# An attention and expert kernel: twelve score tiles in one row, one run of value products behind them

## What is computed

```python
q = (query @ w_q.T).reshape(B, T_q, 16, 8)
k = (kv_source @ w_k.T).reshape(B, T_kv, 16, 8)
v = (kv_source @ w_v.T).reshape(B, T_kv, 16, 8)
attn = softmax(einsum('bqhd,bkhd->bhqk', q, k) * 8 ** -0.5, axis=-1)
out = einsum('bhqk,bkhd->bqhd', attn, v).reshape(B, T_q, 128) @ w_o.T
...
x = x + tanh(g_xattn[0]) * xattn(layernorm(x), ctx)
x = x + tanh(g_ffn[0]) * ffn(layernorm(x))
```

## Time and profile before

| | us |
|---|---|
| three runs | 289.75, 289.96, 289.96; median 289.96 |
| the profiled execution | 289.38 |
| its span (first to last instruction) | 287.6 |
| busy: TensorE, VectorE, ScalarE, GpSimd | 275.9 (96%), 214.9 (75%), 181.9 (63%), 97.5 (34%) |
| attention loop, units 0 to 11 | 26.8 to about 166.6 |
| units 12 and 13 | about 166.6 to 189.9 |
| tail, units 14 and 15 | 189.9 to 209 |
| routing and experts | 209 to 287.6 |

### The profile page before, as it was taken

How to read it: one execution, slowest core, us unless ns; L and a number is a source line. 1 busy time by engine, 2 the same in 40 slices (tenths; PEclk the granted TensorE clock), 3 DMA queues, 4 the chain that set the end, 5 groups by cost and what they waited for, 6 DMA issues and landing times.

```text
span 287.6 us, 8051 instructions
## 1 busy us (share of the span) xinstructions
PE 275.9 (96%) x2826; PEld 222.6 (77%) x2826; DVE 214.9 (75%) x420; ACT 181.9 (63%) x370; POOL 97.5 (34%) x113
## 2 busy tenths in 40 slices
PE   7988999999999999999999998999889999999994
PEld 3465878878878888887887887987688788888862
DVE  5678797797877977979679788797256988877761
ACT  2636776687677776777668666566518778775400
POOL 4598732332062043033233201032600755454200
PEclk9999999999999999999999999999999999999999
DMA  7397945943971990892695499100000000000001
GB/s 252 100 206 194 223 107 167 244 132 102 239 203 17 267 252 1 225 236 76 157 233 147 88 219 309 38 0 2 2 2 0 1 2 0 0 1 0 0 0 32
DMA packets 9924, 32.19 MB, mean 112 GB/s; under 512 B 2576, under 2 KB 3088, under 8 KB 9904
## 3 DMA queue, kind: packets, MB, share of 16 engines
q1 hardware_dynamic: 9472, 31.60, 43.1%
q10 hardware_dynamic: 432, 0.33, 0.3%
HBM read 13.26 MB, written 0.23 MB: 47 GB/s over the span
## 4 chain that ended last, share of the span: by engine, by line
PE 87%; DVE 7%; DMA 2%; ACT 1%; issue 1%; POOL 1%; SPq 0%; DVEq 0%; ACTq 0%
PE max_ps L969 16%; PE score_ps L949 14%; PE o_ps L983 14%; PE misc_ps L937 8%; PE misc_ps L931 5%; PE score_ps L1194 3%; PE score_ps L1196 3%; PE score_ps L1195 3%; DVE part_max L704 2%; PE o_ps L1194 2%; PE o_ps L1280 2%; PE o_ps L1195 2%; PE o_ps L1196 2%; PE max_ps L992 2%; PE misc_ps L1107 1%; PE max_ps L999 1%
## 5 line engine op out<-in xcount | busy, mean ns | idle before, releaser
L704 DVE TENSOR_REDUCE part_max<-max_ps 112x1 f32<-112x512 f32 (+1 forms) x192 | 117.3, 670 | 33.4 <-PE max_ps L969 31.5
L515 ACT ACTIVATE probs<-score_ps 128x448 f32<-128x448 f32 x192 | 92.0, 545 | 16.0 <-PE score_ps L949 15.9
L969 PE MATMUL max_ps<-kx,qx 96*112 96x512 f32 (+1 forms) x192 | 81.9, 432 | 2.2 <-DVE part_max L704 1.1
L949 PEld LDWEIGHTS score_ps<-qx,kx 104*128 104x128 f32 (+1 forms) x384 | 69.1, 188 | 10.7 <-issue 2.1
L949 PE MATMUL score_ps<-qx,kx 104*128 104x224 f32 (+1 forms) x384 | 73.7, 276 | 0.6 <-DVE qx L723 0.4
L983 PE MATMUL o_ps<-probs,v_sb 128*32 128x112 f32 (+1 forms) x1536 | 44.5, 261 | 0.6 <-ACT probs L515 0.6
L969 PEld LDWEIGHTS max_ps<-kx,qx 96*112 96x112 f32 x192 | 33.6, 176 | 8.7 <-issue 4.9
L983 PEld LDWEIGHTS o_ps<-probs,v_sb 128*32 128x32 f32 (+1 forms) x1536 | 36.4, 110 | 3.1 <-ACT probs L515 0.8
L366 POOL TENSOR_TENSOR k_low<-k_full,k_high 128x512 fp32r<-128x512 f32 (+1 forms) x21 | 26.2, 1252 | 30.7 <-ACT k_full L498 30.4
L399 POOL TENSOR_TENSOR o_norm<-o_sb,inv_den 128x112 f32 (+1 forms) x15 | 6.3, 423 | 75.8 <-DVE inv_den L730 75.8
L510 ACT ACTIVATE v_sb<-misc_ps 128x512 f32<-128x512 f32 x24 | 14.4, 601 | 27.4 <-PE misc_ps L937 27.4
(11 more groups left out here) (177 smaller groups left out, 369.0 us busy)
## 6 DMA issues: line engine op xcount, KB each, us to landing
kx<-k_high SPq DMA_DIRECT2D x60, 187.5 KB, 5.2
kx<-k_low SPq DMA_DIRECT2D x30, 187.5 KB, 5.1
ctx_sb<-in_ctxT SPq DMA_DIRECT2D x7, 750.0 KB, 5.7
gu_sb<-in_guT SPq DMA_DIRECT2D x8, 512.0 KB, 5.5
dn_sb<-in_dnT SPq DMA_DIRECT2D x8, 256.0 KB, 5.3
ctx_sb<-in_ctxT SPq DMA_DIRECT2D x2, 256.0 KB, 4.3
kx<-k_high SPq DMA_DIRECT2D x4, 123.5 KB, 2.3
kx<-k_high SPq DMA_DIRECT2D x4, 64.0 KB, 2.0
```

The lines of the kernel that those rows point to most:

```text
L515: nc.scalar.activation(probs[:, (KT * h + t) % 8, :], score_ps[:, t % 3, 0:SC // 2], ACT.Exp, scale=SCALE).then_inc(exp_done, 1)
L704: nc.vector.reduce_max(part_max[:, p, c:c + 1], max_ps[0:PC, bank, 0:size], AX.X).then_inc(max_taken, turns)
L949: last = nc.tensor.matmul(score_ps[0:m, t % 3, GC * g:GC * g + GC], kx[0:KR, 2 * par + h, g, 128 * t:128 * t + m], qx[0:KR, par, 2 * h + g ...
L969: nc.tensor.matmul(max_ps[0:PC, bank, 0:size], qx[0:MR, par, 2 * h + p // 2, PC * (p % 2):PC * (p % 2) + PC], kx[0:MR, slot, p // 2, start ...
```

## The change

On TensorE a unit now has its twelve pairs of a maximum product and a score tile in a row, with only the first job (keys) between the sixth and the seventh. Behind the row come the second job, `denominators`, `transpose_max`, both halves of `attend` without anything between them, and then the third job. `probs` has twelve buffers in place of eight, one for each tile, since tile 0's must live until the row's end. VectorE's order follows: twelve maxima (with `negate_max` after the ninth), and the inversion behind the last of them. ScalarE's follows too: six exponentials, the copy of job one, six exponentials, the copy of job two, `o_copy`, and the copy of job three. In the ring the three products of unit u+2 have turns 9 to 11 and the denominators turn 12 (before: 10 to 12, and 6).

The room for four more tiles of `probs` comes from two places. `k_full` holds two chunks of 512 columns in place of 1536 columns, and the third chunk's copy waits until GpSimd has read the first. `expert_sel`, a table of 16x1024, is gone with VectorE's copy that filled it at the start (L748); GpSimd's `select` reads `row_mask` with a broadcast in its place. The tail, the routing and the experts have the same order as before.

```diff
-DEN, NEXT_ROWS, LATER = 6, 13, 10
+DEN, NEXT_ROWS, LATER = 12, 13, 9
...
-        k_full = sb("k_full", [128, KPAD])
+        k_full = sb("k_full", [128, 2, CK])
...
-        probs = sb("probs", [128, 8, GC * 2])
+        probs = sb("probs", [128, KT, GC * 2])
...
-                nc.gpsimd.tensor_copy(expert_now[:, par, :], expert_sel[:, e, :].bitcast(f32)).then_inc(select_ready, 1)
+                nc.gpsimd.tensor_copy(expert_now[:, par, :], bc(row_mask[:, e].unsqueeze(1), [ROWS, 128])).then_inc(select_ready, 1)
...
-            pool.wait_ge(select_all, 1)
+            pool.wait_ge(rows_ready, 1)
...
                 if whole:
-                    nc.scalar.activation(k_full[:, start:start + size], bank[:, 0:size], ACT.Copy).then_inc(k_saved, 1)
+                    if n == 2:
+                        act.wait_ge(k_low_saved, NCH * b + 1)
+                    nc.scalar.activation(k_full[:, n % 2, 0:size], bank[:, 0:size], ACT.Copy).then_inc(k_saved, 1)
...
                 if jobs[0]:
                     jobs[0](i, par, h, 0)
+                for t in range(RUN, KT):
+                    exp_tile(i, par, h, t)
                 if jobs[1]:
                     jobs[1](i, par, h, 1)
-                for t in range(RUN, KT):
-                    exp_tile(i, par, h, t)
+                o_copy(i, par, h)
                 if jobs[2]:
                     jobs[2](i, par, h, 2)
-                o_copy(i, par, h)
...
-                dve.wait_ge(rows_ready, 1)
-                nc.vector.tensor_copy(expert_sel[:, :, :], bc(row_mask[:, :].unsqueeze(2), [16, E, 128])).then_inc(select_all, 1)
...
-                for n in range(RUN):
-                    take_max(ring(u, n), n % 3, AHEAD + n)
-                invert(u - 1, 1 - h, ring(u, DEN), DEN % 3)
-                for n in range(RUN + AHEAD, UM):
-                    take_max(ring(u, n - 2), (n - 2) % 3, n)
+                for n in range(AHEAD, UM):
+                    take_max(ring(u, n - AHEAD), n % 3, n)
                 negate_max(u + 1, ring(u, LATER))
                 for n in range(AHEAD):
                     take_max(ring(u, LATER + n), (LATER + n) % 3, n)
+                invert(u - 1, 1 - h, ring(u, DEN), DEN % 3)
                 max_rows(ring(u, NEXT_ROWS), NEXT_ROWS % 3, *ahead(i, par, h, 1)[1:], turns=2)
...
                 job(i, par, h, 0)
-                denominators(u - 1, 1 - h, ring(u, DEN), DEN % 3)
-                attend(i, par, h, 0)
-                job(i, par, h, 1)
                 for n in range(RUN + AHEAD, UM):
-                    max_scores(*u1, n, ring(u, n - 2), (n - 2) % 3)
+                    max_scores(*u1, n, ring(u, n - AHEAD), n % 3)
                     scores(i, par, h, n - AHEAD)
                 for n in range(AHEAD):
                     max_scores(*u2, n, ring(u, LATER + n), (LATER + n) % 3)
                     scores(i, par, h, KT - AHEAD + n)
+                job(i, par, h, 1)
+                denominators(u - 1, 1 - h, ring(u, DEN), DEN % 3)
+                transpose_max(u + 1, ring(u, NEXT_ROWS), NEXT_ROWS % 3, turns=2)
+                attend(i, par, h, 0)
+                attend(i, par, h, 1)
                 job(i, par, h, 2)
-                transpose_max(u + 1, ring(u, NEXT_ROWS), NEXT_ROWS % 3, turns=2)
-                attend(i, par, h, 1)
```

More of the change, by code:

```diff
@@ L50 @@
 COMB_MADE = 11
+ROWS = 16
 def chunk(n):
@@ L121, in flamingo_block @@
         scratch = sb("scratch", [128, 1])
-        expert_sel = sb("expert_sel", [16, E, 128], f32r)
         expert_now = sb("expert_now", [16, 2, 128], f32r)
@@ L147, in flamingo_block @@
         zeros = k_high[:, 0, 2 * TOK:2 * TOK + 128]
-        x_expert = k_full[:, 0:TOK]
+        x_expert = k_full[:, 0, 0:TOK]
         hact = probs[:, 0:FT, :]
@@ L153, in flamingo_block @@
         yT = o_flat[:, 2 * TOK:3 * TOK]
-        blank = k_full[:, 0:CK]
-        q_full = [k_full[64:MR, CK * (g - 1):CK * (g - 1) + TOK] for g in (2, 3)]
+        blank = k_full[:, 0, :]
+        q_full = [k_full[64:MR, g - 2, 0:TOK] for g in (2, 3)]
         score_ps = pb("score_ps", [128, 3, 512])
@@ L176, in flamingo_block @@
         kx_loaded = [[sem(f"kx_loaded{u}{g}") for g in range(2)] for u in range(4)]
-        consts, mask_ready, select_all, cleared, pool_step = map(sem, ("consts", "mask_ready", "select_all", "cleared", "pool_step"))
+        consts, mask_ready, cleared, pool_step = map(sem, ("consts", "mask_ready", "cleared", "pool_step"))
         scratch_ready = sem("scratch_ready")
@@ L365, in k_rest @@
                 pool.wait_ge(k_saved, 2 * (NCH * b + n + 1))
-                nc.gpsimd.tensor_tensor(k_low[:, par, start:start + size], k_full[:, start:start + size],
+                nc.gpsimd.tensor_tensor(k_low[:, par, start:start + size], k_full[:, n % 2, 0:size],
                                         k_high[:, par, start:start + size].bitcast(f32), ALU.subtract
@@ L514, in exp_tile @@
                 act.wait_ge(scores_done, KT * unit(i, par, h) + t + 1)
-                nc.scalar.activation(probs[:, (KT * h + t) % 8, :], score_ps[:, t % 3, 0:SC // 2],
+                nc.scalar.activation(probs[:, t, :], score_ps[:, t % 3, 0:SC // 2],
                                      ACT.Exp, scale=SCALE).then_inc(exp_done, 1)
@@ L741, in _, with add_masks @@
             dve.wait_ge(x_loaded, 16)
-            def copy_selectors():
+            def add_masks():
                 dve.wait_ge(heads_ready, 1)
@@ L746, in copy_selectors @@
                                         ALU.add).then_inc(mask_ready, 1)
-                dve.wait_ge(rows_ready, 1)
-                nc.vector.tensor_copy(expert_sel[:, :, :], bc(row_mask[:, :].unsqueeze(2), [16, E, 128])).then_inc(select_all, 1)
-            layer_norm(x_sb, 1, 0, NR, copy_selectors)
+            layer_norm(x_sb, 1, 0, NR, add_masks)
             def q_rest(g):
@@ L984, in attend @@
                                                 v_sb[0:m, par, t, VP * p:VP * p + 32],
-                                                probs[0:m, (KT * h + t) % 8, PC * j:PC * j + PC],
+                                                probs[0:m, t, PC * j:PC * j + PC],
                                                 start=(t == 0), stop=(t == KT - 1), skip_group_check=True)
```

## The result

| | before | after |
|---|---|---|
| median of the runs | 289.86 | 294.19 (293.59 to 295.35) |
| ratio | | 1.0159, interval 1.0126 to 1.0192 |
| profiled execution, its span | 289.38, 287.6 | 293.59, 291.9 |
| busy: TensorE, VectorE, ScalarE, GpSimd | 275.9, 214.9, 181.9, 97.5 | 276.0, 215.1, 177.8, 96.8 |

The account below looks back on a forecast made before the run. TensorE was taken to bound the unit, with VectorE slower inside a row of pairs. Loop +0.7, unit 12 -0.7, unit 13 +0.05, start -0.4 gave -0.35 from 289.96: 289.6 us, range 287.0 to 291.8.

Parts of the forecast that it names:

- The small risk inside the forecast: Every second unit: GpSimd's low part touches `negate_max`'s second step, up to 0.2 per unit, 1.2 in six, 290.8; chance 0.06.
- The wait ahead of `transpose_max`: Loop units: TensorE waits 0.35 us for VectorE's longer chain of maxima before `transpose_max`.
- The value run of 2.42: Twelve value tiles in one run take 2.42 us against 2.61 in two runs, 0.19 less per unit.
- Unit 5 plus unit 6, 0.11 more than before: Loop: unit 5 takes 11.72, 0.07 more; unit 6 takes 11.73, 0.04 more; twelve loop units +0.7 us.
- that the third job's copies run into the next unit and no score tile feels it: ScalarE: copies run to about 1.1; first exponential ends some 1.6, the fourth score tile needing it at 1.7.
- Unit 12, -0.7: Unit without a third job: its absence now saves 0.90, giving -0.8 us, less the 0.07.
- Unit 13, +0.05: Unit with three jobs of the same size: 0.05 us longer.
- The start, -0.4: Program start: removing VectorE's copy into `expert_sel` speeds GpSimd's `rstd`, -0.4 us, bounds 0 and 0.6.
- The late context: Slower rival: context load issued later; landing at 7.2 us holds five units 0.6 each, 292.6; chance 0.12.
- The faster rival: Loop: maxima keep up in the long row, the 0.35 wait goes, units cost 11.37, time 284.7; chance 0.17.
- The sum: Whole kernel: + 0.7 - 0.7 + 0.05 - 0.4 = -0.35, a span of 287.3 and median 289.6 us.
- The range: Whole kernel: 287.0 to 291.8 us, halfway to the faster rival and most of the way to the slower.

Follow-up runs that it names:

- the sixth experiment: Changed kernel with the high part of the negated maxima written by a second reduction in place of the cast, GpSimd not held: 290.14 us, ratio 1.0008.
- the fourth experiment: Changed kernel with GpSimd's staging held until that unit's `negate_max` is done, and `transpose_max` behind both halves of the value products: 287.5 us, ratio 0.9917.
- the third experiment: Kernel before with twelve `probs` buffers, two chunks of `k_full` and no `expert_sel`, but the old order on all engines: 289.45 us, ratio 0.9990.
- the fifth: The fourth experiment with SyncE issuing the first key moves ahead of the context's load instead of behind it: 292.68 us, ratio 1.0115.
- seventh experiments: The fifth experiment with the second reduction of the sixth experiment in place of the cast: 292.47 us, ratio 1.0099.
- the ninth: The fourth experiment with the second job behind the ninth pair of the row on TensorE and ScalarE, instead of behind the twelfth: 287.63 us, ratio 0.9911.
- tenth experiments: The ninth experiment with the reduction of the sixth experiment in place of the cast: 284.9 us, ratio 0.9838.
- the eighth experiment: Kernel before, with GpSimd held so that its staging meets `negate_max` in one unit of every two, six in all: 311.13 us, ratio 1.0728.

## Why the prediction was wrong

- **"The small risk inside the forecast" is the step that failed.** It had the right pair of engines. By the Trainium skill, "SBUF — State Buffer", Who interferes with whom, a VectorE copy or cast in a 2-port mode and a GpSimd instruction exclude each other for a whole instruction, and one with two inputs in SBUF contends with GpSimd's reads. The trace agrees, and puts 1.44 and 0.85 us on it for instructions of 0.17 and 0.16; no row names the cast's mode. The prediction named only the rule on two inputs here, though the step that it set beside GpSimd was the cast, which has one input and took 1.27 of the 1.96. The page's other rule there, that `tensor_reduce` never contends on this chip, agrees with the 0.15 of the reduction in the sixth experiment. What failed was the place and the price. The place: I laid out units 5 and 6 and took them for all of the loop, while in unit 0 GpSimd stages and subtracts right behind its clearing of `kx`, 5.60 into the unit, and not behind the normalising, 10.0 into it. In the odd units GpSimd and the cast pass each other by less than the 0.1 that was said: GpSimd's low part ends at 95.77 in unit 5, and the cast starts at 95.78 and takes 0.17. In all six odd units the two are within 0.01. That nothing was held there is luck, not a margin. The price: "up to 0.2" was about the length of the VectorE instruction. The page speaks of one instruction; in the trace the loser waits for the rest of the other's instruction and for the next one behind it too, for both steps together 1.96; and then, in the profiled execution, TensorE's clock adds 1.63.
- **The wait ahead of `transpose_max`**, forecast 0.35: right, 0.23 to 0.33, and the fourth experiment shows that it is this wait which eats the gain of the long run.
- **The value run of 2.42**: right but for 0.04, 2.46 in one run in place of 1.28 + 1.33 = 2.61 in two before.
- **Unit 5 plus unit 6, 0.11 more than before**: measured 0.20 (23.52 against 23.32). Unit 6 came as laid out: `transpose_max` at 8.25 (109.45 - 101.20; forecast 8.31), the unit 11.72 (forecast 11.73). Unit 5 is the longer one, by 0.1: with its start taken as 88.52 + 0.86, the forecast's length of the job before it, `transpose_max` stands at 8.32 in place of 8.26 and the value run is 0.04 longer. One sentence of that step was wrong, that the third job's copies run into the next unit and no score tile feels it. ScalarE's timeline after, at the start of unit 5:

```profile
89.68 0.60 ACT L495 ACTIVATE k_high<-misc_ps 128x512 fp32r<-128x512 f32 x1 [0.74 <-PE misc_ps L929]
...
90.65 2.73 ACT L517 ACTIVATE probs<-score_ps 128x448 f32<-128x448 f32 x6
```

The first of the six exponentials starts at 90.65 only, and TensorE's fourth score tile, due 0.22 behind the maximum product at 90.81, comes at 91.25: 0.22 late. That this is what puts `transpose_max` 0.06 later was not tried.
- **Unit 12, -0.7**: measured -0.84. **Unit 13, +0.05**: measured +0.01.
- **The start, -0.4**: `rstd` did shrink, by 0.45, and in every kernel without the copy, so the copy was in its way and not the operation's first use. How much of it reaches the loop isn't shown: unit 0 starts 0.12 earlier here and 0.34 earlier in the third experiment, kernels with the same code up to there start it between 26.42 and 27.27, and the third experiment gains 0.3 with an interval that includes nothing. I had counted an instruction's saving on the chain as the chain's saving.
- **The late context**, 292.6, decides at a landing of 6.6: the loads land after up to 6.9, and the one above that cost the 0.3. Right as a mechanism, and small in this kernel; the fifth and seventh experiments show its full size.
- **The faster rival**, VectorE not in the way: wrong. TensorE waits for VectorE's maximum in every unit of the changed kernel, and in the ninth and tenth experiments still at the denominators.
- **The sum.** Forecast -0.35 for the span. Measured +4.3, by the profiled executions: the contact and its clock 3.6, which the sum had at nothing, the loop some 1.7 in place of 0.7, with the late load and other small waits, unit 12 -0.84, the start -0.12.
- **The range** left out that a cost may come in one unit and be large. Its slower side was built of costs that are small and come in five units or more.

## What to carry to other kernels

Where a change moves an instruction on one engine, look at what the engines beside it do at its new time in every unit, the first and the last too, since their queues stand elsewhere there; the steady unit says nothing on them. Price a contact of VectorE with GpSimd by the length of GpSimd's instructions in the queue, not by VectorE's own, and add what an idle TensorE may lose in clock, which it did behind some of these waits and not behind others. Here the long run paid only when the chain that feeds it had a cover as long: GpSimd held back, `transpose_max` behind the run, the second job in the row and a shorter `negate_max` together turned a loss of 4.3 us into a gain of 4.9.

## What the runs showed of the hardware

- A VectorE cast of 112x4 elements, 0.17 us alone, took 1.44, 1.41, 1.60 and 1.58 us beside GpSimd. It was not let in between two GpSimd instructions that follow at once: in the changed kernel it began in the first (32.24 to 33.17) and ended with the second (34.40). A subtraction with two SBUF inputs was held in the same way (0.85 and 1.39 us). A reduction that writes the cast's 112x4 in its place was not held (0.15).
- TensorE's granted clock stood at the 1.2 GHz level for about 3.4 us behind an idle time of 1.68 us in the changed kernel, and stayed at 2.4 GHz behind one of 0.81 us in the sixth experiment. But it also stayed there behind the first idle time of 2.08 us in the eighth, and fell behind the five others of 2.05 to 2.08 us: from the length of the idle time alone these runs can't tell whether the clock falls. The value run of 96 records took 2.46 us at the upper level and 4.09 with the clock low for most of it.
- The six contacts of the eighth experiment cost 3.5 us each on average: 2.1 for the stall, nothing more where the clock held, some 1.4 more where it fell, and 2.9 more once.
